# Attention scores from 48-row float32r stacks, two heads on the two halves of TensorE's rows

## The reference, cut to what matters

```python
x = L0_attn_x                                   # (4, 1024, 256)
xn = _layernorm(x, axis=-1)
s = attention(xn, w_qkv, w_out)                 # 16 heads of 16, causal
g = silu(ffn(xn, W1, B1, W2, B2, LN_G, LN_B))   # 6 blocks, 256 -> 1024 -> 256, exact gelu
return x + s * g

# attention
qkv = (x @ w_qkv).reshape(b, s, 3, 16, 16);  q = q / sqrt(16)
scores = einsum('bqhd,bkhd->bhqk', q, k);    scores = where(causal, scores, -1e10)
out = einsum('bhqk,bkhd->bqhd', softmax(scores), v).reshape(b, s, 256) @ w_out
```

## Time and profile before

| | |
|---|---|
| median of three runs | 1800.6 us |
| span of the profiled execution | 1806.1 us |
| TensorE (products) busy | 1716.2 us, 95% |
| TensorE weight loads busy | 1312.9 us, 73% |
| VectorE busy | 1149.1 us, 64% |
| ScalarE busy | 958.0 us, 53% |
| GpSimd busy | 323.2 us, 18% |
| DMA, mean rate | 54 GB/s |

### The profile page before, as it was taken

One profiled execution on the slowest core, in us unless ns is written; L12 is line 12 of the kernel. 1 busy time (PEld: TensorE's weight loads), 2 busy tenths in 40 slices (PEclk: granted clock), 3 DMA queues, 4 the chain that ended last, 5 costly groups with the idle time before them and its releaser, 6 DMA issues. The chain is left out here.

```text
span 1806.1 us, 33624 instructions
## 1 busy us (share of the span) xinstructions
PE 1716.2 (95%) x11664; PEld 1312.9 (73%) x11664; DVE 1149.1 (64%) x2325; ACT 958.0 (53%) x1364; POOL 323.2 (18%) x317
## 2 busy tenths in 40 slices
PE   6979999999999999999999999997999989999947
PEld 5869999999999989999999998875444433444236
DVE  7846666666666656666666643366877866877326
ACT  5834555555555545555555554432666665666723
POOL 3511111111111111111111111110121211121214
PEclk9989999999999999999999999998999998999969
DMA  6940000000000000000000050003474754574113
GB/s 206 306 140 13 12 17 16 13 12 17 13 9 12 17 16 12 13 17 12 16 12 12 0 83 24 23 24 64 76 112 75 109 84 73 88 107 73 48 57 137
DMA packets 104427, 97.97 MB, mean 54 GB/s; under 512 B 26636, under 2 KB 88588, under 8 KB 104316
## 3 DMA queue, kind: packets, MB, share of 16 engines
q1 hardware_dynamic: 104256, 96.39, 23.9%
q10 hardware_dynamic: 60, 0.10, 0.0%
HBM read 62.15 MB, written 29.62 MB: 51 GB/s over the span
## 5 line engine op out<-in xcount | busy, mean ns | idle before, releaser
L626 ACT ACTIVATE m_hid<-m_h_ps,m_b1s 128x512 f32<-128x512 f32 x384 | 264.3, 688 | 571.0 <-PE m_h_ps L752 558.9
L687 DVE TENSOR_TENSOR m_hidl<-m_hid,m_hidh 128x512 fp32r<-128x512 f32 x384 | 307.4, 809 | 323.9 <-ACT m_hidh L628 322.8
L129 DVE TENSOR_REDUCE mx<-a_s_ps 128x1 f32<-128x512 f32 (+3 forms) x570 | 341.2, 656 | 91.3 <-PE a_s_ps L117 87.8
L1003 ACT ACTIVATE a_prob<-a_st_ps 128x1024 f32<-128x1024 f32 (+1 forms) x320 | 289.9, 938 | 168.5 <-PE a_st_ps L1153 123.0
L752 PE MATMUL m_h_ps<-xth,shared 128*128 (+1 forms) x768 | 269.8, 397 | 12.3 <-DVE shared L655 12.2
L763 PE MATMUL m_y_ps<-shared,m_hidh 128*128 128x256 f32 x1536 | 277.9, 281 | 0.0
L628 ACT ACTIVATE m_hidh<-m_h_ps,m_b1s 128x512 fp32r<-128x512 f32 x384 | 261.8, 682 | 0.0
L763 PEld LDWEIGHTS m_y_ps<-shared,m_hidh 128*128 128x128 f32 x1536 | 246.6, 189 | 12.0 <-DVE m_hidl L687 0.4
L602 POOL TENSOR_TENSOR y<-y,m_b2s 128x1024 f32<-128x1024 f32 x47 | 112.8, 2400 | 708.3 <-DVE y L663 708.3
L763 PE MATMUL m_y_ps<-m_w2h,m_hidh 128*128 128x256 f32 x768 | 217.9, 284 | 0.6 <-DVE m_hidl L687 0.3
L763 PE MATMUL m_y_ps<-shared,m_hidl 128*128 128x256 f32 x768 | 215.8, 281 | 0.0
(11 more groups left out here) (115 smaller groups left out, 2648.3 us busy)
## 6 DMA issues: line engine op xcount, KB each, us to landing
q_parts<-p_part SPq DMA_DIRECT2D x16, 384.0 KB, 3.5
k_parts<-p_part SPq DMA_DIRECT2D x16, 384.0 KB, 3.0
m_raw<-w1t SPq DMA_DIRECT2D x48, 128.0 KB, 2.2
m_raw<-w2t SPq DMA_DIRECT2D x48, 128.0 KB, 2.4
shared<-q_parts SPq DMA_DIRECT2D x48, 128.0 KB, 4.6
shared<-k_parts SPq DMA_DIRECT2D x48, 128.0 KB, 7.7
a_qs<-q_parts SPq DMA_DIRECT2D x48, 128.0 KB, 4.6
a_ks<-k_parts SPq DMA_DIRECT2D x48, 128.0 KB, 7.4
```

The costliest lines, as they stand in the source:

```text
L129: return nc.vector.reduce_max(mx[:, half, first:first + heads, qt], scores, AX_X)
L626: nc.scalar.activation(hid[k % 2][:], h_ps[k % 2][:], ACT.Gelu, bias=b1s[s.par][:, k:k + 1])
L687: nc.vector.tensor_tensor(hidl[k % 4][:], hid[k % 2][:], hidh[k % 4][:].bitcast(F32), ALU.subtract).then_inc(low_done, 1)
L1003: nc.scalar.activation(prob[step % BUFS][:, j:j + heads, 0:hi - lo], unit_ps(unit), ACT.Exp).then_inc(exp_done, 1)
```

## The change

The two parts of q and k are now float32r, the high part from ScalarE and the rest from VectorE; the third part, the rest buffers and GpSimd's step are gone. A stack has 48 rows (q: parts 0, 0, 1; k: 0, 1, 0) and two more for the maximum (`ROWS` = 50). Two heads share the columns: heads 0 and 1 of a group on partitions 0 to 49, heads 2 and 3 on partitions 64 to 113 (`SIDE` = 64), two columns of 1024 each (`PAIR` = 2). Each product has a partner on the other half of the array's rows that writes another PSUM bank.

A piece of the search now fills two banks, one for each side, of the same three; there are 20 pieces with 40 maxima. All products of a piece come first, then all its masks, which still use 128 rows. The bank rule follows: piece p may start when the maxima of piece p-1 have been taken from its first side. A unit of scores is one pair of 512 or 384 columns or two pairs of 256 or 128. The turn has three small VectorE steps; its transpose is float32, and the rows are stored in four DMAs. The loop over batches is written out as 16 bodies. `EARLY` is 6 and `TURN` 4.

```diff
@@ constants
-PARTS = 3
-STACK = 6 * HD
+PARTS = 2
+STACK = 3 * HD
 ROWS = STACK + PARTS
-EARLY = 10
-TURN = 6
+SIDE = P // 2
+PAIR = 2
+EARLY = 6
+TURN = 4
@@ def piece_products(nc, to, q, k, piece, keep):
-    for j in range(heads):
-        i = nc.tensor.matmul(to[:, j, :], q[0:STACK, first + j, qt * P:(qt + 1) * P],
-                             k[0:STACK, first + j, half * BANK:half * BANK + keys], start=True, stop=not diagonal)
-        if diagonal:
-            i = nc.tensor.matmul(to[:, j, keys - P:keys], keep["identb"][:], keep["maskb"][:], start=False, stop=True)
+    for c in range(columns):
+        for side in range(2):
+            rows = slice(SIDE * side, SIDE * side + STACK)
+            i = nc.tensor.matmul(to[side][:, c, :], q[rows, first + c, qt * P:(qt + 1) * P],
+                                 k[rows, first + c, half * BANK:half * BANK + keys], start=(c == 0), stop=not diagonal,
+                                 skip_group_check=True)
+    if diagonal:
+        for c in range(columns):
+            for side in range(2):
+                i = nc.tensor.matmul(to[side][:, c, keys - P:keys], keep["identb"][:], keep["maskb"][:], start=False, stop=True,
+                                     skip_group_check=True)
@@ attend: banks, loop
         def piece_ps(p):
-            return by_head(s_ps[(p + (p >= TURN)) % BANKS], PIECES[p])
+            place = 2 * (p + (p >= TURN))
+            return [by_column(s_ps[(place + side) % BANKS], PIECES[p]) for side in range(2)]
...
-            for hg in range(HG):
-                body(0, hg, hg > 0, 2)
-            with eng.Fori(1, BATCH - 1) as bt:
+            for bt in range(BATCH):
                 for hg in range(HG):
-                    body(bt, hg, True, 2)
-            for hg in range(HG):
-                body(BATCH - 1, hg, True, min(2, HG - 1 - hg))
+                    n = HG * bt + hg
+                    body(bt, hg, n > 0, min(2, N_GROUPS - 1 - n))
@@ store_max (SyncE)
                 for part in range(PARTS):
-                    src = nmt[part * HG * QT:(part + 1) * HG * QT, :]
-                    dst = qs[slot][STACK + part:STACK + part + 1, :, :].rearrange("a h (t q) -> a (h t) q", q=P)
-                    sp.dma_start(dst, src).then_inc(nm_stored, 16)
+                    for side in range(2):
+                        first = part * HG * QT + side * PAIR * QT
+                        row = SIDE * side + STACK + part
+                        dst = qs[slot][row:row + 1, :, :].rearrange("a c (t q) -> a (c t) q", q=P)
+                        sp.dma_start(dst.bitcast(F32), nmt[first:first + PAIR * QT, :]).then_inc(nm_stored, 16)
@@ TensorE: piece, pace, scores
-                if p == TURN + BANKS - 1:
+                if p == TURN:
                     pe.wait_ge(nmt_ready, n + 1)
-                pe.wait_ge(piece_maxed, NP * n + p + (2 if TURN <= p < TURN + BANKS - 1 else 1))
+                pe.wait_ge(piece_maxed, 2 * (NP * n + p) + (1 if p == TURN else 0))
...
-                        now += heads * (keys + (P if qt // HG == half else 0)) + (P if p == NP + TURN else 0)
-                        dve_free = max(dve_free, now + TO_OTHER) + DVE_COLUMN * heads * keys + DVE_START
+                        now += columns * keys + (P if p == NP + TURN else 0)
+                        instructions = 2 * columns if qt // HG == half else 2
+                        dve_free = max(dve_free, now + TO_OTHER) + DVE_COLUMN * 2 * columns * keys + DVE_START * instructions
...
-                    for j in range(heads):
-                        i = nc.tensor.matmul(unit_ps(unit)[:, j, :], ks[hg][0:ROWS, first + j, kt * P:(kt + 1) * P],
-                                             qs[hg][0:ROWS, first + j, lo:hi], start=True, stop=True)
+                    for c in range(columns):
+                        for side in range(2):
+                            rows = slice(SIDE * side, SIDE * side + ROWS)
+                            i = nc.tensor.matmul(unit_ps(unit)[:, side, c, :], ks[hg][rows, first + c, kt * P:(kt + 1) * P],
+                                                 qs[hg][rows, first + c, lo:hi], start=True, stop=True)
@@ project: part 1 and the stores
-                nc.vector.scalar_tensor_tensor(rest[m][:], qk_ps[m][:], 0.25 if m < 2 else 1.0,
-                                               part[m][:, 0, :], ALU.mult, ALU.subtract).then_inc(rest_done, 1)
+                nc.vector.scalar_tensor_tensor(part[m][:, 1, :], qk_ps[m][:], 0.25 if m < 2 else 1.0,
+                                               part[m][:, 0, :].bitcast(F32), ALU.mult, ALU.subtract).then_inc(part1_done, 1)
@@ scratch
-        "q": nc.dram_tensor("q_parts", [DIM, PARTS, TOK], BF16, kind="Internal").ap(),
+        "q": nc.dram_tensor("q_parts", [DIM, PARTS, TOK], F32, kind="Internal").ap(),
```

More of the change, by code:

```diff
@@ L87, in max_pieces @@
             keys = min(P * (qt + 1) - BANK * half, BANK)
-            heads = min(BANK // keys, HG)
-            pieces += [(qt, half, j, heads, keys) for j in range(0, HG, heads)]
+            columns = min(BANK // keys, PAIR)
+            pieces += [(qt, half, c, columns, keys) for c in range(0, PAIR, columns)]
     return pieces
 def load_stacks(sp, scratch, to_q, to_k, bt, hg, loaded):
[L96 to L99, removed]
+    for to, src, order in ((to_q, scratch["q"], (0, 0, 1)), (to_k, scratch["k"], (0, 1, 0))):
+        for side in range(2):
+            first = HG * HD * hg + PAIR * HD * side
+            for r, part in enumerate(order):
+                rows = src[first:first + PAIR * HD, part, bass.ds(SEQ * bt, SEQ)].rearrange("(c d) n -> d c n", d=HD)
+                to_rows = to[SIDE * side + r * HD:SIDE * side + (r + 1) * HD, :, :]
+                sp.dma_start(to_rows.bitcast(F32), rows).then_inc(loaded, 16)
@@ L102, in shared_stacks @@
 def shared_stacks(keep):
[L104 removed]
+    views = [w[:].rearrange("p (c n) -> p c n", n=SEQ) for w in keep["shared"]]
     return views[0:2], views[2:4]
 def piece_products(nc, to, q, k, piece, keep):
[L111 removed]
+    qt, half, first, columns, keys = piece
     diagonal = qt // HG == half
[L113 to L117 removed]
@@ new lines, in piece_products, with by_column, row_max @@
+    if diagonal:
[3 more added lines that the diff above has]
+                                     skip_group_check=True)
+    return i
+def by_column(bank, piece):
+    _, _, _, columns, keys = piece
+    return bank[:, 0:columns * keys].rearrange("p (c n) -> p c n", n=keys)
+def row_max(nc, mx, scores, piece, side):
+    qt, half, first, columns, _ = piece
+    return nc.vector.reduce_max(mx[:, half, PAIR * side + first:PAIR * side + first + columns, qt], scores, AX_X)
@@ L258, in body @@
                 for u in range(2):
[L259 to L263, removed]
+                    if not last:
+                        inverse(2 * p + u + 2, u)
             pairs(pool, body)
@@ L814, in score_units @@
     for step, (_, _, lo, hi) in enumerate(attention_steps()):
-        heads = 2 if hi - lo > BANK // 2 else HG
-        units += [(step, j, heads) for j in range(0, HG, heads)]
+        columns = 1 if hi - lo > BANK // 2 else PAIR
+        units += [(step, c, columns) for c in range(0, PAIR, columns)]
     return units
@@ L997, in body @@
                 n = HG * bt + hg
-                for unit, (step, j, heads) in enumerate(UNITS):
-                    _, _, lo, hi = STEPS[step]
+                for unit, (step, _, _) in enumerate(UNITS):
                     act.wait_ge(st_done, NU * n + unit + 1)
@@ L1144, in scores @@
                     nonlocal now, act_free
-                    step, first, heads = UNITS[unit]
+                    step, first, columns = UNITS[unit]
                     _, kt, lo, hi = STEPS[step]
@@ L1175, in values @@
                     pace(HG * (hi - lo) + P)
-                for unit, (step, first, heads) in enumerate(UNITS):
+                for unit in range(NU):
                     scores(unit)
```

136 lines of the change are left out of this document (61 added, 75 removed).

## The result

The kernel after the change takes 2005.6 us in the median of four runs (1988.5 to 2006.8), against 1801.3 for the kernel before: a ratio of 1.111, interval 1.107 to 1.115. It is slower, as forecast, but by 204 us and not by 103, and outside the stated range of 1822 to 1965.

What follows compares the result with a forecast made beforehand. PE bounded the kernel, at 28.65 us a group. Terms 53.9 (period) + 58.8 (clock) - 13.4 (loop) + 2 (projection) + 2 (first search) gave +103.3 on 1800.6, so 1904 us; range 1822 to 1965, own forecast 1865 to 1950.

Steps and rivals of the forecast that it cites:

- PE sets the period before; products off PE are worth little once VectorE's chain comes last: PE, busy all 28.65 us of an attention group, sets its period; products off it pay until something else comes last.
- Concurrency of the halves: Score pairs on two row halves stream at once, so a group's scores cost 4.4 us instead of 7.8.
- The rival without overlap: Halves do not stream together in score pairs: period 39 us, kernel 1936 us; chance 0.12.
- Turns: Changes between half and full rows around masks: 0.09 us each, 24 of them costing 2.2 us a group.
- the long part: A group up to its last score and piece 18: 19.3 us of PE plus 1.6 of mutual waits with ScalarE.
- The run: Piece 19, then pieces 0 to 5 with the transpose, no other work between: 9.7 us a group.
- The store's wait: First score of the next group waits 1.9 us for the four DMAs that store the maxima.
- The clock: PE falls to 1.2 GHz in the sparse pieces ending a group: 4.2 us a group, +58.8; bounds 0 and 20.
- the loads: float32r weight loads of the two halves not overlapping: no cost taken, bound up to 2.7 us a group.
- The first rival: Clock holds through the sparse pieces ending a group: +44.5 us, 1845 us; chance 0.26.
- The last groups: Last two attention groups, with part of a next search or none: unchanged, bounds 2 us each way.
- The loop: Batch loop written out, so the stall at its branch goes: -13.4 us once, bounds -9 and -13.4.

Runs made afterwards that it cites:

- e6: Kernel after the change with search pieces spread by other placement costs and masks on half rows; 1823.3 us, ratio 1.011.
- e5: Kernel after the change with mask-sized filler products ahead of every wait in the run of pieces at a group's end; 1907.9 us, ratio 1.058.
- e4: Kernel after the change with other costs in the table placing the pieces, so none stand together at a group's end; 1884.1 us, ratio 1.046.
- e2: Kernel before the change with only the loop over batches written out; 1792.1 us, ratio 0.9948.
- e8: e6 with mask-sized filler products ahead of the waits between the MLP and the first score only; 1828.5 us.

## Why the prediction was wrong

- *PE sets the period before; products off PE are worth little once VectorE's chain comes last.* Right. At the full clock and in a good order (e6) a group takes 29.1 us with PE busy 25.8, while the kernel before takes 28.65 with PE busy 28.6. The halving of the score products is real and buys nothing here: VectorE is busy for no less than before (24.2 us of the group for 23.0), and PE waits for it nine times a group, 3.2 us in all.
- *Concurrency of the halves.* Right: the two products of a pair mostly start 3 to 4 ns apart in the trace, and a pair of 512 columns behind another pair takes 0.24 us. The rival without overlap is out.
- *Turns.* Right in sum at 2.3 us for the masks, but a turn has a second part that I missed: the first float32r pair behind strips or masks takes 0.34 us where a following one takes 0.24. In the timeline after, at full clock (1749.26 to 1749.60 behind strips, 1749.60 to 1749.84 behind a pair):

```profile
1749.26 0.50 PE L1153 MATMUL a_st_ps<-a_qs,a_ks 50*128 50x512 f32 x2
1749.60 0.40 PE L121 MATMUL a_s_ps<-shared 48*128 48x512 f32 x2
1749.84 0.34 PE L1153 MATMUL a_st_ps<-a_qs,a_ks 50*128 50x384 f32 x2
```

  The kernel before had no such step, its 256 columns behind strips took 0.12 (1564.09 to the mask at 1564.21). The drain is what the Trainium skill, TensorEngine Tiling (Array Packing), "Key Properties", states, and the trace agrees: a pair takes 0.10 us more up to its mask. The 0.10 for the first pair is this trace's alone. With 16 such entries in the long part (twelve behind strips, four behind masks) it is 1.6 us, about what the long part was short: 22.6 measured in e5, 20.9 forecast.
- *The run.* Right in sum, by two errors that cancel: 12.8 us measured with the wait of 0.42 ahead of piece 19 (13.0 in the mean of the thirteen groups), 12.8 forecast with its share of the low clock. The store's wait in the one shown was 0.67 us and not 1.9 (in another group 2.15), and the rest of it was longer by about that.
- *The clock.* **This is the step that failed**, by its size. "If 6 us of the long part run at the lower level, half of them is lost": it was 4.2 us in the short groups and 22.7 in the long ones, 16.4 in the mean. The long part, up to the wait ahead of piece 19, takes 29.6 us in the mean of the thirteen groups, and 22.6 at full clock (e5): the clock cost it 7.0 us a group, where I had 3.0. I had measured how long a low stretch lasts on one place, though the same trace showed 17 us from the loop's branch on. I gave bounds of 0 and 20 a group for the term and then let the range take in only 1 to 6. With 4.0 us more in fourteen groups the forecast of 1904 would have been 1960, just inside the range; the long part at full clock and the last group, below, carry it to 2005. The range was also narrower than its own terms: with 2.7 for the loads and 6 for the clock it ends at 1967, not at 1950.
- The first rival, that the clock holds, had beside it the Trainium skill, TensorE: Matmul & The Clock Gate, "Why this matters for your kernels", which speaks of a long gap between bursts. The measurement decides against it here: in the kernel after, the clock fell in each of the first fourteen runs with no gap over 0.9 us in the six microseconds ahead of the fall, and in e4 with none over 0.35.
- *The last groups* were set at nothing: the last period took 40.16 us at a clock of 0.65, against 27.1 before and 31.1 in e5, where the clock was 0.98. So it is the clock again, for some 9 of the 13 us.
- *The loop.* Right in kind, 9.8 us by e2 for the forecast's 13.4.

The sum by spans: the change was 198.5 us (2004.6 - 1806.1), the forecast 103.3, so 95.2 short. Thirteen groups x (42.5 - 36.7) are 76, of which 52 are the clock in the long part (7.0 for 3.0), 22 the long part at full clock (22.6 for 20.9) and 2 the run (13.0 for 12.8); the last group is 13, the first 4 (43.5 against 31.7 before, for +8.1 forecast), all else 2. The medians add 6 to that: the profiled execution of the kernel before was 5.5 us over its median. That part of the loop's 13.4 was lengthened by the profile would fit the 9.8 of e2, but no run shows it.

Open stays what decides how long the clock remains low. Groups with the same instructions had 4 and 23 us of it in their long part; from fall to return the clock record of the trace has 14 us in three of the first fourteen, 24 in two and 31 to 34 in nine. That it hits each fourth or fifth group of e4, and one of e8, suggests that the moment of the pauses counts beside their length; no run tests that. Nor was a version of the pair form found that beats the kernel before: e6 comes within 1.1%, and its first group alone takes 46.3 us against 31.7.

## What to carry to other kernels

A change that relieves the engine at full load is worth what the next engine leaves over: find that engine's chain at full clock before counting products. If the change makes TensorE wait, even in pieces of half a microsecond, price the clock for all the dense work behind the waits, as a loss that may come, and take the bounds seriously: the loss is half of a low stretch whose length the waits do not tell. An order table tuned for one form of the work is wrong for another; here four numbers of it were worth 122 us.

## What the runs showed of the hardware

- Work without use can pay: 1818 more products made the kernel 98 us faster (e5), by holding the clock.
- Each side of a mode change shows a price for float32r: 0.10 us to leave (in the kernel after a 512-column pair takes 0.43 from 1753.01 to its mask, with the 0.10 of a first pair in it) and 0.10 more for the first pair behind it. How much of the second part belongs to the mode is not shown: in the MLP of the kernel after, a product on all rows behind masks on all rows also takes 0.20 us where its followers take 0.12. Behind the half-row masks of e6 no such step is seen: two pairs of 128 columns take 0.26 us there (1394.74 to 1395.00), 0.12 each being their price elsewhere. The first rows here are the MLP's:

```profile
1240.16 0.28 PE L127 MATMUL m_tr_ps<-maskb,identb 128*128 128x128 bf16 x2
1240.25 0.36 PE L756 MATMUL m_y_ps<-m_w2h,m_hidh 128*128 128x256 f32 x1
1240.45 0.28 PE L756 MATMUL m_y_ps<-m_w2l,m_hidh 128*128 128x256 f32 x1
```

- Two row halves can take their mask from shifted copies with no mode change, 0.21 us for the mask step of two columns against 0.32. In e6 it goes from 1394.53 to 1394.74, as this timeline shows; in e4 the same step went from 1375.74 to 1376.06:

```profile
1394.25 0.44 PE L122 MATMUL a_s_ps<-shared 48*128 48x128 f32 x4
1394.53 0.40 PE L130 MATMUL a_s_ps<-maskb,identb 64*128 64x128 bf16 x8
1394.74 0.42 PE L1166 MATMUL a_st_ps<-a_qs,a_ks 50*128 50x128 f32 x4
```
